# First attention: two of the four weight transfers of a half unit issued by ScalarE instead of the sync engine

## The chip, the cores and the metric

The kernel runs on one core of one Trainium2 chip. The core has TensorE (matrix products), VectorE, ScalarE and GpSimd, and a sync engine (SP) that mostly issues DMAs; each follows its own list of instructions, and they meet at semaphores. The metric is the device time of one execution in microseconds, less is better.

## The reference, cut to what matters

Two layers, each an attention over a context and a block of experts. Everything below happens in the attention of the first layer:

```python
def _L0_xattn_ref(latents, context, Wq, Wk, Wv, Wo):   # latents 4 x 256 x 512, context 4 x 1601 x 512
    hidden_states = jnp.concatenate([context, latents], axis=1)          # 1857 keys
    q = (latents @ Wq).reshape(b, q_len, N_KV_HEADS, N_GROUPS, HEAD_DIM) # 32 heads of 128
    k = (hidden_states @ Wk).reshape(b, kv_len, N_KV_HEADS, HEAD_DIM)    # 4 heads of keys and values
    v = (hidden_states @ Wv).reshape(b, kv_len, N_KV_HEADS, HEAD_DIM)
    scores = jnp.einsum('bqhgd,bkhd->bhgqk', q, k) * scale
    attn = jax.nn.softmax(scores.astype(jnp.float32), axis=-1)
    out = jnp.einsum('bhgqk,bkhd->bqhgd', attn, v)
    return out.reshape(b, q_len, N_HEADS * HEAD_DIM) @ Wo
...
x = x + _L0_xattn_ref(_layernorm(x), ctx_4096, ...)
x = x + _L0_ffn_ref(_layernorm(x), ...)
x = x + _L1_xattn_ref(_layernorm(x), ctx_4096, ...)
x = x + _L1_ffn_ref(_layernorm(x), ...)
```

## The kernel before, in words

The kernel works through the layers in blocks. The block of the first attention (`grouped_attention_block`) projects queries, keys and values first, then runs the attention proper, then the output projection. Every product is made in three passes with operands split in a high and a low part, so that float32 accuracy is kept.

The attention proper works on 128 **units**: 4 batches times 32 heads. A unit has 256 queries, that is two **half units** j = 0 and j = 1 of 128 queries (one on each partition), and 1857 keys. Each engine runs its own `step`, with instructions of several units interleaved by hand; the first batch and the tail are written out, the other batches are a loop (`run`). SP's list is written out for all units. No planner is at work: what stands in the lists is the order.

One half unit goes like this:

1. TensorE (`scores`) makes 1858 score columns in four banks of PSUM, the first 1024 as score half 0, the other 834 as score half 1. There is one set of banks. It may write half 0 again only once the half unit before has had its first exponential, and half 1 once it has had the second (both through `probs_done`).
2. VectorE (`maximum`, `negate_maximum`) takes the maximum of each score half and, behind both, the negated maximum.
3. ScalarE (`exponentials`) makes the weights: one exponential over 1024 columns, one over 833, each followed by a read of its accumulator (the row's sum). They go to `probs[j][a]`, a being the unit's number modulo 2.
4. The weights must have the keys on the partitions before they can meet the values. For the columns from 1024 on TensorE transposes them (`turn_plain`), ScalarE copies the high part from PSUM (`plain_high`), VectorE subtracts (`plain_low`). For the first 1024 columns it is done in two steps. SP **trades** them (`trade`): four DMAs, each taking a run of 256 columns of all 128 rows to 32 partitions of `traded` (which lies in the space of `xn`). Then VectorE transposes blocks of 32 x 32 out of it (`turn_traded`, four instructions a unit, counted by `turn_done`), ScalarE copies the high part (`turned_high`), GpSimd subtracts (`low`).
5. TensorE multiplies with the values (`weigh_turned`, `weigh_plain`), VectorE copies the output out (`take_output`), SP stores it.

The trade needs only the first exponential. For j = 0 it also waits until all four transposes of the unit two before are done, since they read the half of `traded` that it writes:

```python
sp.wait_ge(probs_done, 4 * u.n + 2 * j + 1)
if j == 0:
    wait(sp, turn_done, TPAIRS * (u.n - 1))
```

In VectorE's list the last of those transposes comes behind the negated maximum of j = 0, behind another transpose, the copy of an output and a low part. SP's list per unit: trade of j = 0, a piece of the next group's keys or values, trade of j = 1, the store of an output, the queries of the unit two ahead. What `trade` brings for a unit is turned by VectorE behind the next unit's second negated maximum.

Of the kernel before, what the change touches and what calls it, by code (L numbers as in the profile page):

```python
# [488 lines left out]
def grouped_attention_block(nc, held, x, ctx_in, wq, wk, wv, wo, x_res, xn, stats, ident, ones):  # L489
# [19 lines left out]
    SQ = 32  # L509
    RUNS = P // SQ  # L510
    RUN = 256
    TURNED = RUNS * RUN
    TBLOCKS = RUN // SQ
    TPAIRS = TBLOCKS // 2
# [15 lines left out]
    with ExitStack() as ctx:  # L530
# [11 lines left out]
        def load_projection(sp, h):  # L542
            sp.dma_start(inv_wide[:, h % 2, :], inv_all[h].partition_broadcast(P)).then_inc(inv_loaded[h % 2], 16)
            sp.dma_start(o_raw[:, h % 2, :], o_all[h]).then_inc(o_loaded[h % 2], 16)
            sp.dma_start(w_raw[:, h % 2, :], wo[HD * h:HD * (h + 1), :]).then_inc(w_loaded[h % 2], 16)

        with ExitStack() as stack:
# [8 lines left out]
            def load_keys(sp, b, g, a, i):  # L556
                sp.dma_start(k_buf[a][:, PIECE * i:PIECE * (i + 1)].bitcast(F32), batch_of(k_all[g], b)[:, PIECE * i:PIECE * (i + 1)]
                             ).then_inc(k_loaded[a], 16)
# [14 lines left out]
            def load_queries(sp, b, h):  # L573
                sp.dma_start(q_buf[:, h % 2, :, :].bitcast(F32), q_all[h, :, :, TOK * b:TOK * (b + 1)]).then_inc(q_loaded[h % 2], 16)
# [13 lines left out]
            probs = [[sb(f"probs{j}{a}", [P, KEYS]) for a in range(2)] for j in range(QT)]  # L588
            traded = xn[:, :, :].rearrange("p t d -> p (t d)")[:, 0:2 * QT * TURNED].rearrange("p (a j g r) -> p a j g r", a=2, j=QT, g=RUNS)
# [12 lines left out]
            s_ps, max_done, neg_max_done, probs_done = sem("s_ps"), sem("max_done"), sem("neg_max_done"), sem("probs_done")  # L602
            sum_done, sum_ps, inv_done, inv_stored = sem("sum_done"), sem("sum_ps"), sem("inv_done"), sem("inv_stored")
            trade_done = [[sem(f"trade_done{j}{a}") for a in range(2)] for j in range(QT)]
            turn_done, t_hi_done, t_done, tv_ps = sem("turn_done"), sem("t_hi_done"), sem("t_done"), sem("tv_ps")
# [6 lines left out]
            def wait(engine, done, count):  # L612

                if not isinstance(count, int) or count > 0:
                    engine.wait_ge(done, count)
# [21 lines left out]
            @block.sync  # L637
            def _(sp):
                def trade(u, j):
                    if not u.live:  # L640
                        return
                    sp.wait_ge(probs_done, 4 * u.n + 2 * j + 1)
                    if j == 0:
                        wait(sp, turn_done, TPAIRS * (u.n - 1))
                    for c in range(RUNS):
                        sp.dma_start(traded[SQ * c:SQ * (c + 1), u.a, j, :, :], probs[j][u.a][:, RUN * c:RUN * (c + 1)]
                                     ).then_inc(trade_done[j][u.a], 16)

                def queries(u):
                    if u.live and u.n >= 2:  # L650
                        sp.wait_ge(s_ps, 4 * (u.n - 1))
                        load_queries(sp, u.batch, u.head)

                def store_output(u):
                    if u.live:
                        sp.wait_ge(copy_done, u.n + 1)
                        sp.dma_start(o_all[u.head][:, TOK * u.batch:TOK * (u.batch + 1)], o_part[:, u.a, :]).then_inc(o_stored[u.a], 16)

                def piece(u):
                    if not u.live or u.n < HPG:  # L660
                        return
                    i = u.head % HPG
                    if i < KPIECES:
                        if i == 0:
                            wait(sp, s_ps, 4 * (u.n - HPG))
                        load_keys(sp, u.batch, u.head // HPG, u.group_a, i)
                    else:
                        if i == KPIECES:
                            wait(sp, tv_ps, TPAIRS * (u.n - KPIECES - HPG))
                            wait(sp, xv_ps, PPAIRS * (u.n - KPIECES - HPG))  # L670
                        for c in VALUE_PIECES[i - KPIECES]:
                            load_values(sp, u.batch, u.head // HPG, u.group_a, c)

                def store_inverses():
                    sp.wait_ge(inv_done, 1)
                    per = P // (QT * HEADS)
                    for b in range(B):
                        rows = slice(QT * HEADS * (b % per), QT * HEADS * (b % per + 1))
                        sp.dma_start(inv_all[:, TOK * b:TOK * (b + 1)].rearrange("h (j t) -> h j t", j=QT),
                                     row_inv[rows, P * (b // per):P * (b // per + 1)]).then_inc(inv_stored, 16)  # L680

                def step(b, r):
                    u = Unit(b, r)
                    trade(u, 0)
                    piece(Unit(b, r + HPG))
                    trade(u, 1)
                    store_output(Unit(b, r - 3))
                    queries(Unit(b, r + 2))
                    if r == UNITS:
                        store_inverses()  # L690
                        sp.wait_ge(inv_stored, 16 * B)
                        for h in range(2):
                            sp.wait_ge(o_stored[h], 16 * (UNITS // 2 - HEADS // 2 + 1))
                            load_projection(sp, h)

                for r in range(UNITS + 3):
                    step(0, r)
                for a in range(2):
                    sp.wait_ge(o_stored[a], 16 * (UNITS // 2))
# [117 lines left out]
            @block.scalar  # L817
            def _(act):
                def exponentials(u, j, half):
                    if not u.live:  # L820
                        return
                    act.wait_ge(neg_max_done, QT * u.n + j + 1)
                    if half == 0:
                        wait(act, trade_done[j][u.a], TRADE * u.use)
                        wait(act, x_ps, PPAIRS * (u.n - 1))
                    lo, hi = HALVES[half]
                    act.activation(probs[j][u.a][:, lo:hi], s_flat[:, lo:hi], ACT.Exp, bias=neg_max[:, j:j + 1], scale=SCALE,  # L827
                                   accum_out=half_sum[:, bass.ds(QT * u.n + j, 1), half]).then_inc(probs_done, 1)

                def turned_high(u, p):  # L830
                    if not u.live:
                        return
                    q, slot = TPAIRS * u.n + p, (TPAIRS * u.r + p) % RING
                    act.wait_ge(turn_done, q + 1)
                    wait(act, tv_ps, q + 1 - RING)
                    act.activation(t_hi[:, slot, :, :], turned[:, slot, :, :], ACT.Copy).then_inc(t_hi_done, 1)  # L836

                def plain_high(u, e):
                    if not u.live:
                        return  # L840
                    q, slot, bank = PPAIRS * u.n + e, (PPAIRS * u.r + e) % PRING, (PPAIRS * u.r + e) % XBANKS
                    m, rows = len(pair_tiles(e)), plain_rows(2 * e)
                    act.wait_ge(x_ps, q + 1)
                    wait(act, xv_ps, q + 1 - PRING)
                    act.activation(x_hi[0:rows, slot, 0:m, :], ps_x[0:rows, bank, 0:TOK * m].rearrange("p (m n) -> p m n", m=m), ACT.Copy  # L845
                                   ).then_inc(x_hi_done, 1)

                def step(b, r):
                    u, v, w = Unit(b, r), Unit(b, r - 1), Unit(b, r - 2)
                    exponentials(v, 1, 0)  # L850
                    plain_high(w, 1)
                    exponentials(v, 1, 1)
                    turned_high(w, 0)
                    turned_high(w, 1)
                    plain_high(w, 2)
                    exponentials(u, 0, 0)
                    plain_high(w, 3)
                    exponentials(u, 0, 1)
                    turned_high(w, 2)
                    turned_high(w, 3)  # L860
                    plain_high(v, 0)

                run(act, step, 4)

            @block.vector
# [1744 lines left out]
```

## Time and profile before

| | |
|---|---|
| Median of 2 runs | 3225.8 us (3225.3 to 3226.3) |
| Profiled execution | 3227.55 us, of which the span from first to last instruction is 3225.8 |
| Mean granted clock of TensorE over the span | 0.974 of full speed |
| Busy over the span | TensorE 3023.2 us (94%), VectorE 2093.0 (65%), ScalarE 1738.8 (54%), GpSimd 963.1 (30%) |
| Trades (line 646) | 1024 DMAs of 128 KB, from 551.5 to 2100.8 us of the span |

The shares are means over stages with different limits; a stage is read by its own windows. Issues of DMAs are shown as the time that they hold the issuing engine's queue, and are not counted as busy.

### The profile page before, as it was taken

What the parts mean: (1) busy time and instruction counts of PE and PEld (TensorE: products, weight loads), DVE (VectorE), ACT (ScalarE), POOL (GpSimd) and SP (SyncE); (2) the same over time, 40 slices, a digit from 0 to 9 for tenths busy, and PEclk for the clock granted to TensorE, in tenths of its full rate; (3) what the DMA queues carried; (4) which work ended last, traced back from release to release, by engine and by line L of the source; (5) the groups of instructions that cost most, each with busy time, mean ns of one, the idle gap of its engine ahead of it and who ended that gap; (6) DMA issues with size and microseconds to landing.
All of it is one profiled execution on the core that took longest, in us unless ns stands there. A gap on an engine that the chain in (4) does not pass through costs nothing. (4 is left out here: it accounts for less than half of the span.)

```text
span 3225.8 us, 53851 instructions
## 1 busy us (share of the span) xinstructions
PE 3023.2 (94%) x18414; PEld 2684.3 (83%) x18414; DVE 2093.0 (65%) x3215; ACT 1738.8 (54%) x3297; POOL 963.1 (30%) x773
## 2 busy tenths in 40 slices
PE   8999998999999999999999999979889798898974
PEld 8888886899999999899998999968668788786763
DVE  4333343788888888788887888844444477665575
ACT  3323343676666666666666666632344455553263
POOL 0000121344444444444443444422100124430144
PEclk9999999999999999999999999999899799998997
DMA  7665685766767776677776676567475211101387
GB/s 250 219 217 193 218 284 191 152 161 162 162 157 161 161 161 158 157 158 162 157 160 156 157 164 152 120 189 241 138 277 166 86 29 41 41 28 33 111 294 250
DMA packets 395364, 522.17 MB, mean 162 GB/s; under 512 B 35356, under 2 KB 292684, under 8 KB 395112
## 3 DMA queue, kind: packets, MB, share of 16 engines
q1 hardware_dynamic: 392552, 510.57, 57.9%
q0 software_dynamic: 2560, 8.39, 0.8%
q8 instruction: 140, 2.29, 0.3%
q14 instruction: 112, 0.92, 0.1%
HBM read 238.15 MB, written 146.46 MB: 119 GB/s over the span
## 5 line engine op out<-in xcount | busy, mean ns | idle before, releaser
L707 POOL TENSOR_TENSOR a_t_lo<-a_turned,a_t_hi 128x512 fp32r<-128x512 f32 x512 | 649.4, 1290 | 939.5 <-ACT a_t_hi L836 939.5
L827 ACT ACTIVATE a_probs<-a_ps_s,a_neg_max 128x1024 f32<-128x1024 f32 (+1 forms) x512 | 529.6, 1034 | 475.3 <-DVE a_neg_max L879 472.5
L872 DVE TENSOR_REDUCE a_half_max<-a_ps_s 128x1 f32<-128x1024 f32 (+1 forms) x512 | 571.1, 1115 | 189.4 <-PE a_ps_s L724 185.2
L722 PE MATMUL a_ps_s<-a_k_buf,a_q_buf 128*128 128x512 f32 (+1 forms) x1024 | 419.9, 410 | 17.9 <-ACT a_probs L827 11.6
L723 PE MATMUL a_ps_s<-a_k_buf,a_q_buf 128*128 128x512 f32 (+1 forms) x1024 | 386.0, 377 | 0.0
L724 PE MATMUL a_ps_s<-a_k_buf,a_q_buf 128*128 128x512 f32 (+1 forms) x1024 | 385.2, 376 | 0.0
L908 DVE TENSOR_TENSOR a_x_lo<-a_ps_x,a_x_hi 128x512 fp32r<-128x512 f32 (+1 forms) x512 | 314.4, 614 | 107.4 <-ACT a_x_hi L845 107.4
L454 DVE TENSOR_TENSOR p_out<-p_ps_j,p_out 128x512 fp32r<-128x512 f32 (+3 forms) x196 | 152.9, 780 | 326.9 <-ACT p_out L383 326.9
L898 DVE STREAM_TRANSPOSE a_turned<-xn 128x512 f32<-128x512 f32 x512 | 357.7, 699 | 1.5 <-POOL a_t_lo L707 1.5
L383 ACT ACTIVATE p_out<-p_ps_j 128x512 fp32r<-128x512 f32 (+3 forms) x196 | 142.1, 725 | 339.5 <-PE p_ps_j L288 339.5
L722 PE MATMUL a_ps_o<-a_t_hi,a_v_buf 128*128 128x256 f32 x1024 | 298.9, 292 | 6.3 <-issue 3.8
L836 ACT ACTIVATE a_t_hi<-a_turned 128x512 fp32r<-128x512 f32 x512 | 298.4, 629 | 2.0 <-DVE a_turned L898 2.0
L845 ACT ACTIVATE a_x_hi<-a_ps_x 128x512 fp32r<-128x512 f32 (+1 forms) x512 | 274.5, 537 | 24.6 <-PE a_ps_x L752 13.0
L723 PE MATMUL a_ps_o<-a_t_lo,a_v_buf 128*128 128x256 f32 x1024 | 287.4, 281 | 0.0
L724 PE MATMUL a_ps_o<-a_t_hi,a_v_buf 128*128 128x256 f32 x1024 | 287.3, 281 | 0.0
L752 PE MATMUL a_ps_x<-a_turn,a_probs 128*128 128x128 f32 (+1 forms) x1792 | 279.1, 272 | 0.0
L722 PE MATMUL a_ps_o<-a_x_hi,a_v_buf 128*128 128x256 f32 (+1 forms) x896 | 262.3, 293 | 0.0
L724 PE MATMUL a_ps_o<-a_x_hi,a_v_buf 128*128 128x256 f32 (+1 forms) x896 | 251.6, 281 | 0.0
L723 PE MATMUL a_ps_o<-a_x_lo,a_v_buf 128*128 128x256 f32 (+1 forms) x896 | 251.3, 281 | 0.0
L752 PEld LDWEIGHTS a_ps_x<-a_turn,a_probs 128*128 128x128 f32 (+1 forms) x1792 | 219.0, 140 | 34.9 <-issue 0.2
L722 PEld LDWEIGHTS a_ps_s<-a_k_buf,a_q_buf 128*128 128x128 f32 x1024 | 195.0, 190 | 49.2 <-issue 11.7
L724 PEld LDWEIGHTS a_ps_s<-a_k_buf,a_q_buf 128*128 128x128 f32 x1024 | 194.5, 190 | 34.2
(373 smaller groups left out, 7094.6 us busy)
## 6 DMA issues: line engine op xcount, KB each, us to landing
xn<-a_probs SPq DMA_DIRECT2D x1024, 128.0 KB, 3.4
a_q_all<-p_out SPq DMA_DIRECT2D x64, 512.0 KB
a_q_buf<-a_q_all SPq DMA_DIRECT2D x128, 256.0 KB, 3.3
a_k_buf<-a_k_all SPq DMA_DIRECT2D x64, 464.5 KB, 4.0
a_v_all<-p_out SPq DMA_DIRECT2D x56, 512.0 KB
d_w_raw<-e_wt_all SPq DMA_DIRECT2D x31, 768.0 KB, 6.2
a_k_all<-p_out SPq DMA_DIRECT2D x48, 384.0 KB
a_v_buf<-a_v_all SPq DMA_DIRECT2D x64, 256.0 KB
```

The costliest lines, as they stand in the source:

```text
L454: dve.tensor_tensor(job_views(n, 1)[0], ps, hi.bitcast(F32), ALU.subtract).then_inc(job_done, 1)
L707: pool.tensor_tensor(t_lo[:, slot, :, :], turned[:, slot, :, :], t_hi[:, slot, :, :].bitcast(F32), ALU.subtract).then_inc(t_done, 1)
L722: pe.matmul(o, w_hi, m_hi, start=first, stop=False)
L723: pe.matmul(o, w_hi, m_lo, start=False, stop=False)
L724: return pe.matmul(o, w_lo, m_hi, start=False, stop=last)
L752: tr = pe.transpose(ps_x[0:rows, bank, col:col + P], probs[j][u.a][:, c0:c0 + rows], turn[:, :])
L827: act.activation(probs[j][u.a][:, lo:hi], s_flat[:, lo:hi], ACT.Exp, bias=neg_max[:, j:j + 1], scale=SCALE, accum_out=half_sum[:, bass.ds( ...
L836: act.activation(t_hi[:, slot, :, :], turned[:, slot, :, :], ACT.Copy).then_inc(t_hi_done, 1)
L845: act.activation(x_hi[0:rows, slot, 0:m, :], ps_x[0:rows, bank, 0:TOK * m].rearrange("p (m n) -> p m n", m=m), ACT.Copy).then_inc(x_hi_don ...
L872: dve.reduce_max(half_max[:, half:half + 1], s_flat[:, lo:hi], AX.X).then_inc(max_done, 1)
L898: dve.transpose(turned[:, slot, :, :].rearrange("p k (q r) -> p k q r", r=SQ), traded[:, u.a, :, :, 2 * SQ * p:2 * SQ * (p + 1)].rearrange ...
L908: dve.tensor_tensor(x_lo[0:rows, slot, 0:m, :], ps_x[0:rows, bank, 0:TOK * m].rearrange("p (m n) -> p m n", m=m), x_hi[0:rows, slot, 0:m, ...
```

## The change

ScalarE gets a `trade` of its own, with the same two waits, which issues the last two of the four DMAs; SP keeps the first two. In ScalarE's list it stands between the two exponentials of the half unit, behind the copy that already stood there. Data, sizes, destinations and semaphores are the same.

```diff
@@ SP @@
-                    for c in range(RUNS):
+                    for c in range(RUNS // 2):
                         sp.dma_start(traded[SQ * c:SQ * (c + 1), u.a, j, :, :], probs[j][u.a][:, RUN * c:RUN * (c + 1)]
                                      ).then_inc(trade_done[j][u.a], 16)
@@ ScalarE @@
+                def trade(u, j):
+                    if not u.live:
+                        return
+                    act.wait_ge(probs_done, 4 * u.n + 2 * j + 1)
+                    if j == 0:
+                        wait(act, turn_done, TPAIRS * (u.n - 1))
+                    for c in range(RUNS // 2, RUNS):
+                        act.dma_start(traded[SQ * c:SQ * (c + 1), u.a, j, :, :], probs[j][u.a][:, RUN * c:RUN * (c + 1)]
+                                      ).then_inc(trade_done[j][u.a], 16)
@@ ScalarE, step @@
                     exponentials(v, 1, 0)
                     plain_high(w, 1)
+                    trade(v, 1)
                     exponentials(v, 1, 1)
...
                     exponentials(u, 0, 0)
                     plain_high(w, 3)
+                    trade(u, 0)
                     exponentials(u, 0, 1)
```

ScalarE in the middle of the attention, from the first exponential of j = 1 to the second of j = 0, before (`a_probs` are the weights, `a_x_hi` and `a_t_hi` high parts, `a_ps_s` the scores, `a_ps_x` transposed weights):

```order
L827 ACTIVATE a_probs,a_half_sum<-a_ps_s,a_neg_max 128x1024 [waits a_x_ps,a_trade_done10,a_neg_max_done]
L845 ACTIVATE a_x_hi<-a_ps_x 128x512 [waits a_xv_ps,a_x_ps]
L827 ACTIVATE a_probs,a_half_sum<-a_ps_s,a_neg_max 128x833 [waits a_neg_max_done]
L836 ACTIVATE a_t_hi<-a_turned 128x512 [waits a_tv_ps,a_turn_done] x2
L845 ACTIVATE a_x_hi<-a_ps_x 128x512 [waits a_xv_ps,a_x_ps]
L827 ACTIVATE a_probs,a_half_sum<-a_ps_s,a_neg_max 128x1024 [waits a_x_ps,a_trade_done01,a_neg_max_done]
L845 ACTIVATE a_x_hi<-a_ps_x 65x256 [waits a_xv_ps,a_x_ps]
L827 ACTIVATE a_probs,a_half_sum<-a_ps_s,a_neg_max 128x833 [waits a_neg_max_done]
```

The same stretch of ScalarE now:

```order
L827 ACTIVATE a_probs,a_half_sum<-a_ps_s,a_neg_max 128x1024 [waits a_x_ps,a_trade_done11,a_neg_max_done]
L855 ACTIVATE a_x_hi<-a_ps_x 128x512 [waits a_xv_ps,a_x_ps]
L837 DMA xn<-a_probs 32x4x256 [waits a_probs_done]
L837 DMA xn<-a_probs 32x4x256
L827 ACTIVATE a_probs,a_half_sum<-a_ps_s,a_neg_max 128x833 [waits a_neg_max_done]
L846 ACTIVATE a_t_hi<-a_turned 128x512 [waits a_tv_ps,a_turn_done] x2
L855 ACTIVATE a_x_hi<-a_ps_x 128x512 [waits a_xv_ps,a_x_ps]
L827 ACTIVATE a_probs,a_half_sum<-a_ps_s,a_neg_max 128x1024 [waits a_x_ps,a_trade_done00,a_neg_max_done]
L855 ACTIVATE a_x_hi<-a_ps_x 65x256 [waits a_xv_ps,a_x_ps]
L837 DMA xn<-a_probs 32x4x256 [waits a_turn_done,a_probs_done]
L837 DMA xn<-a_probs 32x4x256
L827 ACTIVATE a_probs,a_half_sum<-a_ps_s,a_neg_max 128x833 [waits a_neg_max_done]
```

Two issues now stand ahead of each exponential over 833 columns, with a wait for ScalarE's own first exponential, and for j = 0 with one for VectorE's transposes as well. SP over one unit, before (`a_k_buf` and `a_q_buf` are keys and queries):

```order
L646 DMA xn<-a_probs 32x4x256 [waits a_turn_done,a_probs_done]
L646 DMA xn<-a_probs 32x4x256 x3
L557 DMA a_k_buf<-a_k_all 128x929
L646 DMA xn<-a_probs 32x4x256 [waits a_probs_done]
L646 DMA xn<-a_probs 32x4x256 x3
```

SP over the same unit now:

```order
L646 DMA xn<-a_probs 32x4x256 [waits a_turn_done,a_probs_done]
L646 DMA xn<-a_probs 32x4x256
L557 DMA a_k_buf<-a_k_all 128x929
L646 DMA xn<-a_probs 32x4x256 [waits a_probs_done]
L646 DMA xn<-a_probs 32x4x256
```

SP keeps its waits and its place, and issues two of each four.

## Rows read from the trace of the kernel before

**Rows 1.** Busy time by windows: PE, PEld, DVE, ACT, POOL, PE clock, DMA share, GB/s.

```profile
800.00:1600.00 800.00, 797.32 (x5480) 734.83 (x5479) 647.40 (x990) 550.47 (x1057) 334.83 (x264) 1.00 0.72 160
...
2300.00:2700.00 400.00, 345.94 (x1972) 295.76 (x1971) 215.64 (x385) 189.21 (x384) 60.65 (x57) 0.91 0.37 124
```

**Rows 2.** Waits of PE, 700 to 2300 us: total us, times, longest.

```profile
PE a_ps_o L722 <- issue: 3.8, 2, 1.9
...
PE a_ps_s L722 <- ACT a_probs L827: 1.4, 2, 0.8
```

**Rows 3.** Timeline of a half unit j = 0: start, us, engine, line, operation.

```profile
1399.23 1.12 ACT L827 ACTIVATE a_probs<-a_ps_s,a_neg_max 128x1024 f32<-128x1024 f32 x1 [1.85 <-DVE a_neg_max L879]
...
1400.24 0.19 ACT L827 ACTIVATION_READ_ACCUMULATOR a_probs<-a_ps_s,a_neg_max  x1
...
1400.40 0.69 DVE L898 STREAM_TRANSPOSE a_turned<-xn 128x512 f32<-128x512 f32 x1
...
1400.49 0.50 PE L722 MATMUL a_ps_s<-a_k_buf,a_q_buf 128*128 128x512 f32 x1
...
1400.60 0.95 ACT L827 ACTIVATE a_probs<-a_ps_s,a_neg_max 128x833 f32<-128x833 f32 x1
...
1401.16 2.49 SPq L646 DMA_DIRECT2D xn<-a_probs  x4
...
1401.44 0.20 ACT L827 ACTIVATION_READ_ACCUMULATOR a_probs<-a_ps_s,a_neg_max  x1
...
1402.24 2.54 POOL L707 TENSOR_TENSOR a_t_lo<-a_turned,a_t_hi 128x512 fp32r<-128x512 f32 x2 [3.28 <-ACT a_t_hi L836]
1402.30 0.19 PEld L722 LDWEIGHTS a_ps_s<-a_k_buf,a_q_buf 128*128 128x128 f32 x1
...
1402.68 0.60 ACT L845 ACTIVATE a_x_hi<-a_ps_x 128x512 fp32r<-128x512 f32 x1
...
1403.41 0.31 PE L724 MATMUL a_ps_s<-a_k_buf,a_q_buf 128*128 128x322 f32 x1
...
1403.76 1.02 DVE L872 TENSOR_REDUCE a_half_max<-a_ps_s 128x1 f32<-128x833 f32 x1
...
1404.28 0.28 PE L722 MATMUL a_ps_o<-a_t_hi,a_v_buf 128*128 128x256 f32 x1
...
1404.82 0.21 DVE L879 TENSOR_SCALAR a_neg_max<-a_half_max 128x1 f32<-128x1 f32 x1
```

**Rows 4.** Timeline of the half unit j = 1 behind it.

```profile
1405.16 1.12 ACT L827 ACTIVATE a_probs<-a_ps_s,a_neg_max 128x1024 f32<-128x1024 f32 x1 [1.87 <-DVE a_neg_max L879]
...
1406.17 0.19 ACT L827 ACTIVATION_READ_ACCUMULATOR a_probs<-a_ps_s,a_neg_max  x1
...
1406.39 3.36 SPq L646 DMA_DIRECT2D xn<-a_probs  x4
...
1406.42 0.60 ACT L845 ACTIVATE a_x_hi<-a_ps_x 128x512 fp32r<-128x512 f32 x1
...
1406.91 0.95 ACT L827 ACTIVATE a_probs<-a_ps_s,a_neg_max 128x833 f32<-128x833 f32 x1
...
1407.75 0.20 ACT L827 ACTIVATION_READ_ACCUMULATOR a_probs<-a_ps_s,a_neg_max  x1
...
1408.24 0.19 PEld L722 LDWEIGHTS a_ps_s<-a_k_buf,a_q_buf 128*128 128x128 f32 x1
...
1411.27 1.12 ACT L827 ACTIVATE a_probs<-a_ps_s,a_neg_max 128x1024 f32<-128x1024 f32 x1 [1.75 <-DVE a_neg_max L879]
```

**Rows 5.** Line 646, the trades: duration of an issue, and time to landing.

```profile
L646 SPq DMA_DIRECT2D xn<-a_probs x1024: 547/602/2113, 551.5 to 2100.8; - x171
...
DMA to landing us min/median/max: 2.7/3.4/5.4
```

**Rows 6.** Waits of SP's queue, 800 to 2200 us.

```profile
SPq L615 <- DVE a_turned L898: 311.5, 107, 3.8
```

**Rows 7.** The shortest kind of issue on SP, in the output projection.

```profile
2227.95 0.32 SPq L543 DMA_DIRECT2D a_inv_wide<-a_inv_all  x1
```

## Prediction

> **What bounds the kernel now.** I read the stages by their windows first, then TensorE's waits in the first attention, and then one unit of it instruction by instruction, because the edit lies in that loop alone.
>
> In the middle of the first attention TensorE is busy 797 of 800 us at the full clock, and ScalarE 550, VectorE 647 [rows 1]. So TensorE is the bound, and in the whole stretch it waited for the exponentials only twice, 1.4 us in all [rows 2]. That small number is easily misread as distance. Rows 3 and 4 show two consecutive half units, from one first exponential to the next: 1399.23 to 1405.16 for j = 0 and 1405.16 to 1411.27 for j = 1, 12.04 us a unit. In them runs a loop that touches TensorE: second score half ends, VectorE takes its maximum and negates it, ScalarE does the first exponential (1024 columns) and the second (833 columns), and only then may TensorE write the second score half of the next half unit.
>
> Its slack is what TensorE has left when it gets there. For j = 0 the second exponential is complete, with its accumulator read, at 1401.44 + 0.20 = 1401.64, and the score weights that need its banks load at 1402.30 [rows 3]. TensorE's answer to such a release takes some 0.06 us (first exponential complete at 1400.24 + 0.19 = 1400.43, first score half from 1400.49). That leaves 0.60 us. For j = 1 it is 1408.24 - (1407.75 + 0.20) - 0.06 = 0.23 us [rows 4]. Anything over 0.60 and 0.23 us that comes between the first and the second exponential stops TensorE.
>
> **The change part by part.** *Taken from SP:* two of four issues per half unit. An issue takes 0.602 us in the median and a run of four 2.49 [rows 3, 5]. What does this free? The copies land 3.4 us after issue [rows 5], while VectorE turns them only after both halves of the next unit are scored, and a unit is 12.04 us long; TensorE's longest waits in the loop name the exponentials and nothing that moves data, and 3.8 us have no releaser [rows 2]. So earlier issue or landing is worth 0 us, with those 3.8 as the ceiling.
>
> *Added to ScalarE:* the same two issues, between its two exponentials, 256 half units. ScalarE's own idle time does not pay for them: it comes later in the half unit, before the next first exponential, 1.87 us that end at 1405.16 [rows 4]; the issues stand earlier, on the loop. What hides them is the copy from PSUM that stands between the first exponential and the issue (it is queued ahead, and runs while ScalarE's queue waits and issues), plus the slack above. The trace has no DMA issue on ScalarE, so its price is bounded by SP's rows: 0.32 us, the shortest kind of issue [rows 7], 0.547 for the shortest of this kind [rows 5], and 3.36 / 4 = 0.84 for one of a run that had to queue [rows 4]. I take 2.49 / 4 = 0.62: same instruction, same shape, and the run of rows 3. Two make 1.24 us. After them the second exponential has to be started; from the negated maximum's end (1404.82 + 0.21 = 1405.03) to ScalarE's start at 1405.16 that takes 0.13 us, which I add.
>
> *Added waits.* For j = 1 ScalarE waits for its own first exponential, which is complete before SP starts at 1406.39 [rows 4]. No new delay. For j = 0 it also waits for VectorE's four transposes of the unit two before, since the target buffer is theirs. On SP that wait held up only SP (107 waits, 311.5 us in the stretch [rows 6]). On ScalarE the second exponential is queued behind it, and TensorE's second score half behind that. The last transpose ends at 1400.40 + 0.69 = 1401.09, SP starts at 1401.16, but ScalarE starts its second exponential today at 1400.60 [rows 3]: over half a microsecond earlier.
>
> *Sum for j = 0:* new start 1401.16 + 1.24 + 0.13 = 1402.53, against 1400.60: 1.93 us late, less 0.60 of slack, stops TensorE for 1.33 us. *For j = 1:* 1406.39 + 1.24 + 0.13 = 1407.76 against 1406.91: 0.85 late, less 0.23, stops it for 0.62 us.
>
> Does a stop come back? The maximum starts where the second score half ends (last matmul 1403.41 + 0.31 = 1403.72, maximum 1403.76 [rows 3]), and the rest of the loop follows it, so the whole pattern moves by the stop and the next half unit has its old slack again. No engine gets idle time that shortens it. Nor does another link go first: VectorE's transposes come off the same negated maximum, and ScalarE's last copy before the next first exponential, which ends at 1402.68 + 0.60, moves by 1.93 to 1405.21 [rows 3], while the negated maximum that it must not hold up moves to 1405.03 + 1.33 = 1406.36. The nearest is GpSimd: its first low part, the first of two in 2.54 us from 1402.24, so done by 1403.51, is wanted at 1404.28 [rows 3]; it moves 1.93 and TensorE 1.33, which leaves 0.17 of that 0.77.
>
> The transposes are waited for in 126 units (all but the first two), and 127 second halves of j = 1 are followed by another score half: 126 x 1.33 + 127 x 0.62 = 168 + 79 = 246 us. The profiled execution took 3227.55 us (its span 3225.8, and 1.75 around it), 0.05% above the median of the runs, so its own time becomes 3474, and the same 246 on the median of 3225.8 gives **3472 us**, 7.6% more. A unit then lasts 12.04 + 1.95 = 14.0 us.
>
> With x for ScalarE's two issues, the stops are x + 0.09 and x - 0.62 (none below 0). At x = 1.09 (0.547 each) the sum is 208 us, 3434; at 1.68 (0.84 each) it is 358, 3584. That is this case's own range.
>
> **The rivals.** *A: the two issuers share what makes the descriptors.* Then ScalarE's two issues lie between SP's two, which start from the same semaphore, and take up to SP's four, 2.49 us; the stops are 2.58 and 1.87, 126 x 2.58 + 127 x 1.87 = 563 us: 3788. With three of the four ahead, x = 1.86: 403 us, 3629. For it: single issues of this line reached 2.113 us [rows 5], so something behind SP can hold it. Against it: most runs of four take the same 2.49, and nothing in this trace issues from two sequencers at once. The Trainium skill speaks for it ("Perfetto Trace Analysis", section "DMA Instruction — HWDGE (DVE, Sync)"): the block that generates descriptors is shared by the two sequencers that issue such DMAs, is locked for one at a time, and the profiled duration holds the wait for the lock. No row here can show a lock wait, since one engine issues.
>
> *B: not slower. An issue holds ScalarE hardly at all.* If ScalarE hands the issue on and goes to the second exponential at once, x is near 0, j = 1 costs nothing (x - 0.62 is negative) and j = 0 only its wait for the transposes: 126 x 0.09 = 11 us, 3237. The point from which it decides: 2% is 64.5 us, reached at 126 (x + 0.09) = 64.5, x = 0.42, or 0.21 us an issue. Against it: no issue row here is that short, the shortest kind being 0.32 [rows 7], which would give 94 us, 3320. For it: SP has nothing but such work, so its rows can't show what a compute engine's queue hides. The Trainium skill leans this way ("DMA: Bandwidth & Descriptors", section "Issuing engines are not separate DMA queues"): what issuing from several engines saves is the sequencer's initiation time, and that is usually small relative to the DMA. Here the row decides: 0.62 us is not small beside slacks of 0.60 and 0.23.
>
> *C: faster.* SP, relieved of 2.5 us a unit, would have to bring forward a load that TensorE waits for. Rows 2 name none; at most 3.8 us, 3222, inside what cannot be told.
>
> That the change does not do what it says is excluded by the order of instructions: the issues stand on ScalarE ahead of the 833-column exponential.
>
> **How the numbers follow.** Forecast 0.68, A 0.17, B 0.13, C 0.02. The range has to leave out no more than 0.2: it takes the forecast's 3434 to 3584, goes up to 3640 for an A in which the issuers only partly hold each other (half of its chance), and down to 3320 for an issue of 0.32 us (a third of B's): 3320 to 3640. A measurement of this kernel tells about 2% from no change. Slower by more: forecast, A and the dear end of B, 0.87; within: the rest of B and most of C, 0.11; faster 0.02.
>
> **What would show it.** Right: two issue rows of about 0.6 us on ScalarE in each half unit; the second exponential starting 1.9 us (j = 0) and 0.85 us (j = 1) later after the first than now; TensorE's wait for the exponentials grown from 1.4 us to some 250; a unit of 14.0 us; everything outside the first attention unchanged. A shows as issue rows over 1 us on both engines. B shows as the second exponential starting while the issues still run. The forecast would also be wrong if TensorE's clock gave way in the gaps: it is at 1.00 here, but 0.91 in a later stretch where TensorE is busy 346 of 400 us [rows 1], about the share of 12 in 14 that I expect here. Both score halves lie on the loop, so that would add to the time; I leave it inside the upper end.

## The result, and the profile after

The changed kernel takes 3586.7 us (median of 2 runs, 3585.7 to 3587.7) against 3225.8: a ratio of 1.1113 with a 95% interval of 1.1095 to 1.1131, so 361 us slower. The forecast was 3472, with a range of 3320 to 3640. Sign, mechanism and range held; the size was 246 instead of 361. The measured time lies 3 us above 3584, the end of the forecast's own range, and so in the part that was added for an A in which the issuers only partly hold each other.

Where the time went is told by windows cut at the first and last trade. Columns: window, its length, busy time of PE, PEld, DVE, ACT and POOL, PE clock, DMA share, GB/s. Of the kernel before:

```profile
0.00:551.50 551.50, 533.74 (x2604) 461.20 (x2604) 207.24 (x293) 196.22 (x303) 42.66 (x43) 0.99 0.67 226
551.50:2100.80 1549.30, 1536.11 (x10508) 1413.46 (x10508) 1245.36 (x1902) 1059.76 (x2033) 639.34 (x504) 1.00 0.70 156
2100.80:3225.80 1125.00, 953.30 (x5302) 809.68 (x5302) 640.42 (x1021) 482.78 (x963) 281.10 (x226) 0.93 0.41 138
```

And of the kernel after:

```profile
0.00:553.00 553.00, 534.53 (x2604) 461.66 (x2604) 207.48 (x293) 195.89 (x302) 42.65 (x43) 0.99 0.66 226
553.00:2459.00 1906.00, 1621.06 (x10503) 1439.72 (x10504) 1244.69 (x1901) 1068.89 (x2032) 639.38 (x504) 0.98 0.65 127
2459.00:3586.00 1127.00, 954.27 (x5309) 811.22 (x5308) 641.68 (x1022) 483.61 (x965) 281.30 (x226) 0.93 0.41 138
```

All but 4 us lies in the attention proper: 1549 us have become 1906, while what ScalarE and VectorE have to do there stayed at 1060 to 1069 and 1245 us. TensorE, 797 of 800 us busy before [rows 1], has got holes: 285 us without work in the attention, where it had 13. Its busy time for the same work has grown too, by 85 us (1536 to 1621). Its waits, 700 to 2600 us of the kernel after, answer to [rows 2] (total us, times, longest):

```profile
PE a_ps_s L722 <- ACT a_probs L827: 256.6, 235, 2.5
...
PE a_ps_o L722 <- issue: 4.8, 2, 2.8
```

1.4 us and 2 times have become 256.6 and 235, and nothing else in the attention waits more than 1 us longer than before. The 256.6 look like the "some 250" that the forecast gave as a sign, but the loss is 361: this row doesn't count all of a stop. TensorE's weight loads, which come ahead of the matmuls, show more of it. Their waits over the attention, of the kernel before (551 to 2101 us) and after (553 to 2459 us):

```profile
PEld a_ps_s L722 <- ACT a_probs L827: 8.9, 9, 2.9
```

```profile
PEld a_ps_s L722 <- ACT a_probs L827: 338.9, 256, 3.0
```

That is 330 us more. The other 27 or so of the 357 are an estimate for TensorE working slower, at a mean granted clock of 0.98 instead of 1.00. The next rows are the timeline of one unit of the kernel after, first j = 1 and then j = 0; they answer to [rows 3] and [rows 4].

```profile
760.20 1.12 ACT L827 ACTIVATE a_probs<-a_ps_s,a_neg_max 128x1024 f32<-128x1024 f32 x1 [1.27 <-DVE a_neg_max L891]
...
761.43 1.19 SPq L646 DMA_DIRECT2D xn<-a_probs  x2
761.50 0.60 ACT L855 ACTIVATE a_x_hi<-a_ps_x 128x512 fp32r<-128x512 f32 x1
761.51 1.40 ACTq L837 DMA_DIRECT2D xn<-a_probs  x2
...
762.96 0.96 ACT L827 ACTIVATE a_probs<-a_ps_s,a_neg_max 128x833 f32<-128x833 f32 x1 [0.85 <-issue]
...
764.06 0.19 PEld L722 LDWEIGHTS a_ps_s<-a_k_buf,a_q_buf 128*128 128x128 f32 x1 [0.62 <-ACT a_probs L827]
764.06 0.50 PE L722 MATMUL a_ps_s<-a_k_buf,a_q_buf 128*128 128x512 f32 x1 [0.39 <-ACT a_probs L827]
...
766.81 1.12 ACT L827 ACTIVATE a_probs<-a_ps_s,a_neg_max 128x1024 f32<-128x1024 f32 x1 [1.28 <-DVE a_neg_max L891]
...
768.22 0.69 DVE L910 STREAM_TRANSPOSE a_turned<-xn 128x512 f32<-128x512 f32 x1
...
768.99 1.20 SPq L646 DMA_DIRECT2D xn<-a_probs  x2
769.00 1.47 ACTq L837 DMA_DIRECT2D xn<-a_probs  x2
...
770.52 0.96 ACT L827 ACTIVATE a_probs<-a_ps_s,a_neg_max 128x833 f32<-128x833 f32 x1 [2.24 <-issue]
...
771.62 0.19 PEld L722 LDWEIGHTS a_ps_s<-a_k_buf,a_q_buf 128*128 128x128 f32 x1 [1.51 <-ACT a_probs L827]
```

In j = 1 ScalarE's issues run from 761.51 to 762.91 and its second exponential starts at 762.96, 2.76 us after the first; before it was 1406.91 - 1405.16 = 1.75 [rows 4]. In j = 0 the issues can start only when VectorE's transpose has ended at 768.91, and the second exponential is 3.71 us behind the first, before 1.37 [rows 3]. TensorE's weight load for the second score half shows what this does to it: it stood for 0.62 and 1.51 us, where the forecast had 0.62 and 1.33 (the matmul's row counts only 0.39 of the first). That the 0.62 agree is chance: the second exponential of this j = 1 came later than forecast, and the mean loss of a half unit j = 1 is larger (117 us over 127 of them in e2 below, 0.92 each). Line 837 is ScalarE's trade, line 646 SP's (duration of an issue in ns, least, median, most; then time to landing):

```profile
L837 ACTq DMA_DIRECT2D xn<-a_probs x512: 554/625/2324, 553.1 to 2458.7; - x171
...
DMA to landing us min/median/max: 2.9/4.3/5.6
```

```profile
L646 SPq DMA_DIRECT2D xn<-a_probs x512: 547/556/1824, 553.1 to 2458.6; - x171
...
DMA to landing us min/median/max: 2.9/3.5/4.9
```

The median of 0.625 is close to SP's 0.602 [rows 5], but it mixes two things: the first issue of a pair takes 0.57 us, the second 0.87 (j = 0) and 0.77 (j = 1) in the median (timeline rows, 700 to 1900 us). ScalarE's transfers land later than SP's did, not sooner. What SP was relieved of it waits away. Its waits for VectorE's transposes grew from 311.5 us [rows 6] to (800 to 2500 us):

```profile
SPq L615 <- DVE a_turned L910: 586.8, 110, 8.5
```

### The profile page after: what moved, and what is told of

It is laid out like the page before. It is cut to its first block and busy times, and to the rows that moved or that the text cites. A ratio compares the mean times of both kernels' runs of the same rounds, so it can differ in the third digit from the quotient of the medians.

```text
span 3585.9 us, 53935 instructions
## 1 busy us (share of the span) xinstructions
PE 3109.9 (87%) x18414; PEld 2712.6 (76%) x18414; DVE 2093.9 (58%) x3215; ACT 1748.4 (49%) x3297; POOL 963.3 (27%) x773
## 5 line engine op out<-in xcount | busy, mean ns | idle before, releaser
L722 PE MATMUL a_ps_o<-a_t_hi,a_v_buf 128*128 128x256 f32 x1024 | 306.9, 300 | 8.7 <-issue 4.8
L724 PE MATMUL a_ps_o<-a_t_hi,a_v_buf 128*128 128x256 f32 x1024 | 290.5, 284 | 0.0
L722 PE MATMUL a_ps_o<-a_x_hi,a_v_buf 128*128 128x256 f32 (+1 forms) x896 | 267.6, 299 | 0.0
L724 PE MATMUL a_ps_o<-a_x_hi,a_v_buf 128*128 128x256 f32 (+1 forms) x896 | 256.3, 286 | 0.0
```

What stands on the lines that cost most here:

```text
L722: pe.matmul(o, w_hi, m_hi, start=first, stop=False)
L724: return pe.matmul(o, w_lo, m_hi, start=False, stop=last)
```

## The experiments

Seven kernels. One reading serves them all, so it stands here: the mean time from the start of a unit's first exponential (1024 columns) to the start of its second (833 columns), over the timeline rows from 700 to 1900 us. By the forecast's argument a unit loses what this time has grown by, less the slack of 0.60 us (j = 0) or 0.23 (j = 1), 126 and 127 times. "By the gaps" is that sum; "measured" is median minus median of the kernel before in the same comparison.

| kernel | gap j = 0 | gap j = 1 | by the gaps, us | measured, us | ratio (95%) |
|---|---|---|---|---|---|
| before | 1.37 | 1.79 | | | |
| changed | 3.82 | 3.04 | 233 + 130 = 363 | 361 | 1.1113 (1.1095 to 1.1131) |
| e1 waits only | 2.15 | 1.84 | 23 + 0 | 15 | 1.0047 (1.0030 to 1.0064) |
| e2 j = 1 only | 1.37 | 2.97 | 0 + 121 | 117 | 1.0365 (1.0344 to 1.0385) |
| e3 j = 0 only | 3.81 | 1.97 | 232 + 0 | 249 | 1.0773 (1.0751 to 1.0794) |
| e4 SP later | 3.56 | 2.78 | 200 + 97 = 297 | 295 | 1.0918 (1.0894 to 1.0942) |
| e5 all four | 4.92 | 4.80 | 372 + 353 = 725 | 790 | 1.2454 (1.2411 to 1.2497) |
| e6 late place | 1.37 | 1.80 | 0 | 5 | 1.0018 (1.0007 to 1.0029) |
| e7 one issue | 2.78 | 2.09 | 102 + 9 = 111 | 97 | 1.0306 (1.0277 to 1.0334) |

The theory is that the loss is the delay of the second exponential beyond TensorE's slack, made of a wait and of the time that issues hold ScalarE. The rivals: the wait itself is what costs; an issue costs wherever it stands; the two issuers hold each other (A).

**e1, the waits without the issues.**

```diff
-for c in range(RUNS // 2):          # SP
+for c in range(RUNS):
-for c in range(RUNS // 2, RUNS):    # ScalarE
+for c in range(0):
```

> ScalarE keeps both waits between its exponentials but issues nothing; SP issues all four transfers. If the loss is the time that the issues hold ScalarE, only the wait for the transposes of j = 0 is left: a stop of about 0.1 us in 126 units, 11 us, 3237 us. If waiting itself is dear (ScalarE has to let its own exponential finish and to start again twice a unit), the second exponential starts 0.3 us or more later in both halves and the time is 3260 to 3330 us.

3241.7 us against 3226.6. So the two waits alone cost 15 us, and without the issues there is no large loss. Beside the issues the wait for the transposes costs more, since it has used up the slack that would hide a part of them. If the issues of j = 0 started as early behind the first exponential as those of j = 1 do in the changed kernel (1.51 instead of 2.09 us in the mean), it would lose 126 x 0.58 = 73 us less; that is an estimate, and no run here has the issues without the wait. One half unit j = 0 of its timeline:

```profile
999.74 1.12 ACT L827 ACTIVATE a_probs<-a_ps_s,a_neg_max 128x1024 f32<-128x1024 f32 x1 [1.67 <-DVE a_neg_max L891]
...
1001.06 0.69 DVE L910 STREAM_TRANSPOSE a_turned<-xn 128x512 f32<-128x512 f32 x1
...
1001.92 0.96 ACT L827 ACTIVATE a_probs<-a_ps_s,a_neg_max 128x833 f32<-128x833 f32 x1 [0.71 <-issue]
```

The transpose ends at 1001.75 and ScalarE goes on 0.17 us later. It ends 2.01 us after the first exponential's start, where rows 3 had 1.86, so the gap is 2.18 instead of the 2.06 that the forecast's numbers make without issues. The slack takes most of it.

**e2 and e3, one half of the change each.**

```diff
-for c in range(RUNS // 2):                            # SP, e2
+for c in range(RUNS if j == 0 else RUNS // 2):
-trade(u, 0)                                           # ScalarE's step, e2
...
-for c in range(RUNS // 2):                            # SP, e3
+for c in range(RUNS if j == 1 else RUNS // 2):
-trade(v, 1)                                           # ScalarE's step, e3
```

> Only the half units j = 1 are shared with ScalarE; j = 0 is as before. If each half unit pays for its own delay, this costs what the trace of the changed kernel shows for j = 1: the second exponential 2.99 instead of 1.74 us behind the first on average, less 0.23 of slack, 127 times, 130 us: 3355 us. If the two delays make each other worse (TensorE's clock giving way in the gaps, transfers piling up), it costs less than that: by the forecast's 0.62 us a stop 79 us, 3305 us.

> Only the half units j = 0 are shared with ScalarE; j = 1 is as before. If each half unit pays for its own delay: 3.83 instead of 1.37 us between the exponentials, less 0.60 of slack, 126 times, 234 us: 3460 us, and with the kernel that shares j = 1 alone the two losses add up to the whole 361. If they make each other worse, the forecast's 1.33 us a stop, 168 us: 3394 us.

3343.5 and 3475.1 us: 117 and 249 us, together 366 against 361. The two halves add up; neither makes the other worse by an amount that shows. In e2 the untouched half unit keeps its gap (1.37). In e3 that of j = 1 grows from 1.79 to 1.97: inside its slack of 0.23 on the mean, but in some half units beyond it. Summed half unit by half unit these come to 18 us, about the 17 that the table lacks for e3.

**e4, ScalarE's issues without SP's beside them.**

```diff
-sp.wait_ge(probs_done, 4 * u.n + 2 * j + 1)
+sp.wait_ge(probs_done, 4 * u.n + 2 * j + 2)
```

> As changed, but SP waits for the second exponential before it issues its two, so that ScalarE issues its two alone. If the two issuers hold each other (a shared block), the pair on ScalarE falls from a mean of 1.4 to 1.6 us with some over 2 to the 1.2 us that two take on SP alone, and the time by 0.3 us a half unit, to about 3500 us. If an issue on ScalarE is dearer by itself, the pair stays at 1.35 to 1.47 us in the median, and the time within 2% of 3587 us.

3522.0 us; a ratio to before of 1.0918 where the changed kernel has 1.1113, which is 63 us less. ScalarE's pair in j = 0:

```profile
720.76 1.21 ACTq L837 DMA_DIRECT2D xn<-a_probs  x2
722.02 0.96 ACT L827 ACTIVATE a_probs<-a_ps_s,a_neg_max 128x833 f32<-128x833 f32 x1 [1.98 <-issue]
...
723.09 1.20 SPq L646 DMA_DIRECT2D xn<-a_probs  x2
```

The median pair falls from 1.47 us (j = 0) and 1.35 (j = 1) in the changed kernel to 1.21 in both, which is what two take on SP (1.20 in the third row). So rival A is right in kind and small in size: beside SP's issues ScalarE's pair takes 0.14 to 0.26 us more, not 1.25 more. SP's own pair is not slowed: 1.20 us in the median in the changed kernel, 1.19 here. What e4 does not remove are single long pairs, 1.6 to 2.45 us: 17 of 84 pairs of j = 0 here between 700 and 1900 us, 19 of 80 in the changed kernel.

**e5, all four on ScalarE.**

```diff
-for c in range(RUNS // 2):          # SP
+for c in range(0):
-for c in range(RUNS // 2, RUNS):    # ScalarE
+for c in range(RUNS):
```

> ScalarE issues all four transfers of a half unit between its exponentials and SP none. If what makes the issues dearer than 0.62 us is SP issuing at the same time, four take some 2.45 us, the second exponential starts 4.67 (j = 0) and 3.85 us (j = 1) after the first, and the time is 126 x 2.70 + 127 x 1.88 = 579 us over the kernel before, 3806 us, up to 3855 with the occasional long issue. If ScalarE's issues are dearer by themselves (0.73 each), four take 2.92 us and it is some 110 us more, 3915 us or above.

4018.4 us, above both expectations. The issues went as the first of them said, 2.55 to 2.58 us for four in the median (means 2.69 and 2.83). What was missing in these expectations is TensorE's clock. Its windows, in the same columns as above, over 800 us and over 4 us, and the stop that the latter begin with:

```profile
800.00:1600.00 800.00, 623.65 (x3633) 559.71 (x3631) 430.01 (x658) 367.99 (x700) 219.72 (x175) 0.89 0.47 106
```

```profile
1000.00:1002.00 2.00, 0.90 (x2) 0.81 (x3) 0.00 (x0) 1.99 (x5) 0.35 (x1) 0.71 1.09 282
1002.00:1004.00 2.00, 2.00 (x9) 1.81 (x9) 0.41 (x1) 0.57 (x2) 2.00 (x2) 0.50 0.52 96
```

```profile
1001.11 0.80 PE L722 MATMUL a_ps_s<-a_k_buf,a_q_buf 128*128 128x512 f32 x1 [2.38 <-ACT a_probs L827]
...
1006.54 0.60 ACT L855 ACTIVATE a_x_hi<-a_ps_x 128x512 fp32r<-128x512 f32 x1 [0.43 <-PE a_ps_x L752]
1006.54 2.75 ACTq L837 DMA_DIRECT2D xn<-a_probs  x4
```

The granted clock over these 800 us of the attention is 0.89. After the stop of 2.38 us TensorE runs at 0.50, which is 1.2 instead of 2.4 GHz. Its late transposes then hold up ScalarE's copy, and the issue behind it (1006.54 for both): in j = 1 the first issue starts 2.00 us behind the first exponential in the mean, against 1.51 in the changed kernel. The gaps account for 126 x (4.92 - 1.37 - 0.60) + 127 x (4.80 - 1.79 - 0.23) = 725 of the 790 us; that the other 65 are score halves made at the lower clock is an argument, not shown by a run.

**e6, the same issues in another place.**

```diff
 exponentials(v, 1, 0)
 plain_high(w, 1)
-trade(v, 1)
 exponentials(v, 1, 1)
 turned_high(w, 0)
 turned_high(w, 1)
 plain_high(w, 2)
+trade(v, 1)
 exponentials(u, 0, 0)
 plain_high(w, 3)
-trade(u, 0)
 exponentials(u, 0, 1)
 turned_high(w, 2)
 turned_high(w, 3)
 plain_high(v, 0)
+trade(u, 0)
```

> As changed, but ScalarE issues its two at the end of its half unit, behind the copies and just ahead of its wait for the next negated maximum, where it has 1.75 to 1.87 us of idle time; number, size and waits are the same. If the loss comes from the place (on the loop that the second exponential closes), a pair of 1.2 to 1.5 us and 0.13 us hide there, and the time is that of the kernel before, 3226 us, up to 3250 for long issues that reach over the idle time. If issuing from ScalarE costs wherever it stands (its transfers disturb the other engines, or late transfers hold up VectorE's transposes), most of the 361 us stay: over 3400 us.

3233.7 against 3228.3 us. The same 512 issues, the same waits, and the 361 us are down to 5.

```profile
1005.40 0.56 ACTq L837 DMA_DIRECT2D xn<-a_probs  x1
...
1005.60 0.58 ACT L855 ACTIVATE a_x_hi<-a_ps_x 128x512 fp32r<-128x512 f32 x1
1005.98 0.62 ACTq L837 DMA_DIRECT2D xn<-a_probs  x1
...
1008.01 1.12 ACT L827 ACTIVATE a_probs<-a_ps_s,a_neg_max 128x1024 f32<-128x1024 f32 x1 [1.83 <-DVE a_neg_max L891]
```

ScalarE still idles 1.83 us before its first exponential, as in [rows 4], because the issues run in that time and partly beside a copy. So the issues as such and their later transfers cost at most the few us that are left (2 to 9 by the interval); the place on the loop costs the rest. And relieving SP brought nothing: this is no faster than the kernel before.

**e7, one issue instead of two.**

```diff
-for c in range(RUNS // 2):          # SP
+for c in range(RUNS - 1):
-for c in range(RUNS // 2, RUNS):    # ScalarE
+for c in range(RUNS - 1, RUNS):
```

> ScalarE issues one transfer of the four, SP three. If the loss is the time on the loop beyond the slack, then with 0.62 to 0.73 us for the issue j = 0 loses 0.83 to 0.94 us and j = 1 0.01 to 0.12: 106 to 134 us, 3332 to 3360 us, far less than half of the loss for j = 1. If the loss is in proportion to the issues, it is half of 361: 3407 us.

3325.3 us, 97 us more than before: not in proportion (181), but what is left above the slack, a little under the 106 to 134 expected. ScalarE's issues:

```profile
L837 ACTq DMA_DIRECT2D xn<-a_probs x256: 554/568/685, 552.4 to 2197.7; - x128
```

A single issue takes 0.57 us and never more than 0.69, though SP issues three at the same time. So in a pair of 1.47 it is the second issue that takes longer, some 0.9 us by difference.

## Why the prediction was right, and where it was too small

*What bounds the kernel, and the loop.* Right. The stops sit where they were placed, on the score half that waits for the second exponential, and the sums by the gaps and by the slacks of 0.60 and 0.23 us come within 2 to 17 us of seven of the eight measured losses.

*Taken from SP: nothing.* Right as far as SP's relief goes; e6 has it without the loss, and gains nothing. No run has transfers that land earlier, so that an earlier landing would gain nothing is the forecast's argument alone.

*Added waits.* Right in size for the wait alone: 11 us were forecast, e1 measured 15. For j = 1 "no new delay" was wrong: ScalarE's issue there waits for the copy ahead of it (below).

*The price of the issues.* This is the larger of the two terms that were mis-sized. 0.62 us an issue was right for most issues that run alone (e4: 1.21 us a pair in the median). The forecast took it from SP's rows, where nothing runs beside, and gave the rival in which the two issuers hold each other a chance of its own instead of a part in the sum. Both hold: with SP's pair beside it ScalarE's median pair is 1.47 and 1.35 us, with means of 1.61 and 1.41. It also took a typical run where a mean was needed: SP's runs of four in the kernel before take 2.49 us in the median but 2.76 in the mean (700 to 1900 us), since some issues are long. Issues over 1 us, which the forecast named as the sign of A, are not one: 75 of the 1024 were that long before, 80 after. The Trainium skill's rule cited in the forecast ("Perfetto Trace Analysis", section "DMA Instruction — HWDGE (DVE, Sync)": one issuer at a time holds the shared block) fits e4, where ScalarE's pair falls to 1.21 us; but single issues beside SP's took 0.57 us (e7), so if it is this block, it cannot be held for the whole of an issue.

*The sum.* 115 us were missing. In gaps: 3.82 instead of 3.30 for j = 0, and 3.04 instead of 1.79 + 0.85 = 2.64 for j = 1, which is 126 x 0.52 + 127 x 0.40 = 116 us. Two terms make them up (means of the changed kernel, 700 to 1900 us). The pairs are longer than the 1.24 us of the forecast by 0.37 and 0.17: 126 x 0.37 + 127 x 0.17 = 68 us. And the first issue starts later behind the first exponential than the forecast had it, 2.09 instead of 1.93 us and 1.51 instead of 1.23: 126 x 0.16 + 127 x 0.28 = 56 us. (Together 124; the kernel before has a mean gap of 1.79 in j = 1 where rows 4 have 1.75, which takes off 5. The sums are means times counts, so they meet the 116 only roughly.)

e4 gives back 63 of the 115, so that much is SP's issues beside ScalarE's, with what follows from them (granted clock 0.99 over 800 to 1600 us instead of 0.98). The other 50 or so are what remains in e4, which took 3522 us where 3472 had been forecast: 126 x (3.56 - 3.30) + 127 x (2.78 - 2.64) = 51. Two parts of that can be named. The transposes that j = 0 waits for end 0.15 us later behind the first exponential than in rows 3 (e1). Half of that was there before: SP's trade of j = 0 starts 2.01 us behind the first exponential in the median of the kernel before, and rows 3, where it is 1.93, show a unit in which it was early. And some pairs are long, or start late: the mean gap of j = 0 in e4 is 3.56, its median 3.45.

Why every few units an issue takes up to 1.7 us more is open. It isn't SP's trade beside it, since e4 keeps the long ones, and SP alone had them before (3.36 for four [rows 4]). It isn't ScalarE either: of the 42 second issues over 1 us that ScalarE has in the changed kernel, 38 end within 0.05 us of one of SP's that is as long. Whatever holds them holds both.

*What the forecast overlooked about the order in ScalarE's queue.* It let the copy ahead of the issues run beside them. It does, but the issue starts only when the copy's own wait for TensorE is over. Mostly that costs 0.1 us (761.43 on SP, 761.51 on ScalarE). When TensorE is late it costs more, as here in the changed kernel, where a long pair of j = 0 stops TensorE and the j = 1 behind it starts its issues 1.23 us after SP:

```profile
826.31 2.19 ACTq L837 DMA_DIRECT2D xn<-a_probs  x2
...
829.65 0.50 PE L722 MATMUL a_ps_s<-a_k_buf,a_q_buf 128*128 128x512 f32 x1 [1.98 <-ACT a_probs L827]
...
832.72 1.11 ACT L827 ACTIVATE a_probs<-a_ps_s,a_neg_max 128x1024 f32<-128x1024 f32 x1 [1.60 <-DVE a_neg_max L891]
...
833.95 1.19 SPq L646 DMA_DIRECT2D xn<-a_probs  x2
...
835.17 0.60 ACT L855 ACTIVATE a_x_hi<-a_ps_x 128x512 fp32r<-128x512 f32 x1 [1.25 <-PE a_ps_x L752]
835.18 1.22 ACTq L837 DMA_DIRECT2D xn<-a_probs  x2
...
836.44 0.96 ACT L827 ACTIVATE a_probs<-a_ps_s,a_neg_max 128x833 f32<-128x833 f32 x1 [0.67 <-issue]
```

*TensorE's clock.* The forecast named it as a risk inside the upper end. It fell from 1.00 to 0.98 over the attention, and the case above is one of its episodes: after the stop of 1.98 us that ends at 829.65, the windows of the next 4 us have 0.63 and 0.52.

```profile
830.00:832.00 2.00, 2.00 (x10) 1.91 (x9) 0.59 (x1) 1.12 (x3) 1.81 (x2) 0.63 1.03 230
832.00:834.00 2.00, 2.00 (x12) 2.00 (x11) 1.87 (x4) 1.21 (x2) 0.71 (x1) 0.52 0.07 24
```

## What to carry to other kernels

An engine that is 54% busy over the span, with 1.8 us idle in every half unit, can still have no time at the point where work is put: read the slack of the loop behind that very place, and move the work to where the idle time is. A DMA issue on ScalarE was an instruction of over half a microsecond in its list here, and it brought its waits, and those of the instruction ahead of it, onto what stood behind. Before work is taken off a queue, look for someone who waits for that queue; here nobody did.

## What the runs showed of the hardware that was not expected

- Where SP and ScalarE issue at the same time, ScalarE's pair is slowed, but little: 1.21 us in the median for a pair alone, 1.35 to 1.47 beside SP's pair, 0.57 for a single one beside three. SP's pair isn't: 1.19 and 1.20.
- On ScalarE a DMA issue is not passed by the exponential behind it (issues to 836.40, exponential from 836.44), and it does not pass the wait of the copy ahead of it, but runs beside that copy (835.17 and 835.18 above).
- Some issues are up to 1.7 us longer than the others of their kind (75 of 1024 over 1 us in the kernel before), with one issuer or two. The cause is open.
- With stops of 1.94 us in the median ahead of the score matmuls, 64 of 131 of them 2 us or more, TensorE's granted clock is 0.89 on average (e5, 800 to 1600 us); with a median of 1.25 us, 9 of 162 of 2 us or more (the changed kernel), it is 0.98. (Stops of 700 to 1900 us.)
